# A selective-scan stage whose loop runs over batches instead of over batch and scan order

## What is computed

```python
x_dbl = einsum('bkdl,kcd->bkcl', xs, x_proj_w)         # -> dts (6), Bs (16), Cs (16)
delta = softplus(einsum('bkrl,kdr->bkdl', dts, dt_projs_w) + dt_projs_b)
A = -exp(A_logs)                                       # (K, 192, 16)
h = exp(delta * A) * h + (delta * u) * B               # 4096 steps, state 192 x 16
y = einsum('bkdn,bkn->bkd', h, C) + D * u
```

## Time and profile before

| | us |
|---|---|
| median of 3 runs (lowest, highest) | 13187.52 (13180.49, 13191.48) |
| the profiled execution's own time | 13188.5 |
| its span, first to last instruction | 13186.6 |
| scan stage, first to last recurrence | about 925 to 11000 |

### The profile page before, as it was taken

How to read it: one execution, slowest core, us unless ns; L and a number is a source line. 1 busy time by engine, 2 the same in 40 slices (tenths; PEclk the granted TensorE clock), 3 DMA queues, 4 the chain that set the end, 5 groups by cost and what they waited for, 6 DMA issues and landing times. The chain is left out here.

```text
span 13186.6 us, 117417 instructions
## 1 busy us (share of the span) xinstructions
PE 8944.7 (68%) x25624; PEld 2522.6 (19%) x25624; DVE 11097.4 (84%) x7002; ACT 7096.2 (54%) x9476; POOL 9937.2 (75%) x4196
## 2 busy tenths in 40 slices
PE   7866666666666666666666666666666664777777
PEld 2211111111111111111111111111111111222222
DVE  7769999999999999999999999999999995333333
ACT  6755555555555555555555555555555552444444
POOL 0029999999999999999999999999999994211220
PEclk9977777777777777777777777777777776888888
DMA  4567777777777777777777777777777784323230
GB/s 140 166 184 172 175 176 179 175 173 173 177 177 177 175 172 178 177 176 176 172 171 176 175 177 177 172 176 177 177 177 173 175 180 105 78 61 83 65 81 24
DMA packets 581902, 2060.69 MB, mean 156 GB/s; under 512 B 82662, under 2 KB 87654, under 8 KB 566886
## 3 DMA queue, kind: packets, MB, share of 16 engines
q1 hardware_dynamic: 581478, 2057.01, 68.1%
HBM read 1599.54 MB, written 457.18 MB: 156 GB/s over the span
## 5 line engine op out<-in xcount | busy, mean ns | idle before, releaser
L819 POOL TENSOR_TENSOR dBu<-rep,BC 128x1024 f32<-128x1024 f32 x3072 | 7152.8, 2354 | 963.0 <-DMA rep<-dd_dram 922.2
L615 PE MATMUL py<-hC,fold 128*32 128x512 f32 x12288 | 2958.3, 861 | 2587.5 <-POOL hC L826 2443.7
L664 ACT ACTIVATE pd<-rep,a_now 128x1024 f32<-128x1024 f32 x3072 | 3420.9, 1114 | 1326.4 <-DVE hC L787 1002.3
L779 DVE TENSOR_TENSOR_SCAN pd<-pd,carry,dBu 128x1024 f32<-128x1024 f32 x1536 | 3595.5, 2341 | 0.0
L826 POOL TENSOR_TENSOR hC<-h,BC 128x1024 f32<-128x1024 f32 x1024 | 2400.5, 2344 | 531.9 <-DVE h L779 484.7
L787 DVE TENSOR_TENSOR hC<-pd,BC 128x1024 f32<-128x1024 f32 x2048 | 2507.5, 1224 | 169.6 <-DVE pd L779 29.2
L779 DVE TENSOR_TENSOR_SCAN h<-pd,carry,dBu 128x1024 f32<-128x1024 f32 x768 | 1797.9, 2341 | 0.0
L676 ACT ACTIVATE carry<-pd 128x1 f32<-128x1 f32 x1536 | 262.0, 171 | 2630.2 <-DVE hC L787 2582.3
L615 PEld LDWEIGHTS py<-hC,fold 128*32 128x32 f32 x12288 | 516.8, 138 | 4803.9 <-POOL hC L826 3205.8
L779 DVE TENSOR_TENSOR_SCAN pd<-pd,dBu 128x1024 f32<-128x1024 f32 x512 | 1168.0, 2281 | 43.4 <-issue 28.3
L1385 POOL TENSOR_TENSOR p_yn<-p_yn,p_z 96x1024 f32<-96x1024 f32 x64 | 149.8, 2345 | 1192.3 <-DMA p_z<-zs_dram 774.8
(11 more groups left out here) (147 smaller groups left out, 9216.5 us busy)
## 6 DMA issues: line engine op xcount, KB each, us to landing
rep<-dd_dram SPq DMA_DIRECT2D x1024, 768.0 KB, 12.7
BC<-bc_dram SPq DMA_DIRECT2D x2048, 256.0 KB, 9.1
u_dram<-p_u SPq DMA_DIRECT2D x64, 1536.0 KB, 16.7
u<-u_dram SPq DMA_DIRECT2D x128, 768.0 KB, 5.4
dd_dram<-LG SPq DMA_DIRECT2D x256, 384.0 KB, 4.5
dd_dram<-RL SPq DMA_DIRECT2D x256, 384.0 KB, 3.0
y_dram<-y SPq DMA_DIRECT2D x256, 384.0 KB, 10.9
p_y<-y_dram SPq DMA_DIRECT2D x64, 1536.0 KB, 13.9
```

The lines of the kernel that those rows point to most:

```text
L615: last = mm(py[32 * g:32 * g + 32, t2(t)], fold[:, :], hC[:, j % 2 * 3 + g, t2(t)], start=(j % 4 == 0), stop=(j % 4 == 3), skip_group_chec ...
L664: go(pd[:, i % 2, :], rep[:, half, 0, g, :], ACT.Exp, scale=a_now[:, i:i + 1]).then_inc(S.exped, 1)
L779: v.tensor_tensor_scan(dst, pd[:, i % 2, :], dBu[:, i % 4, :], carry[:, i:i + 1] if c else 0.0, ALU.mult, ALU.add).then_inc(S.scanned, 1)
L819: nc.gpsimd.tensor_tensor(dBu[:, i % 4, :], rep[:, half, 1, g, :], BC[:, s, 0, r, :], ALU.mult).then_inc(S.dbu, 1)
```

## The change

The loop now runs over 7 batches. Its body has the four orders and so 16 chunks written out; the last batch, with its 4 orders, stands behind the loop. The bodies get the order's number `k` as a plain number, and `pick_a` uses it for the column of `a_neg`, whose address is then fixed and not computed from the loop's register. One `sem_inc` that stood between a wait and the copy in `pick_a` goes away. Of the 31 passages between orders, 6 are now jumps, 24 lie inside the written-out code and one leads out of the loop.

```diff
         def chunk_loop(eng, body):
 
-            with eng.Fori(0, BK - 1) as bk:
+            with eng.Fori(0, B - 1) as b:
+                for k in range(K):
+                    for c in range(NC):
+                        body(b * K + k, k, c, NC)
+            for k in range(K):
                 for c in range(NC):
-                    body(bk, c, NC)
-            for c in range(NC):
-                body(BK - 1, c, NC - 1 - c)
+                    body(BK - K + k, k, c, NC if k < K - 1 else NC - 1 - c)
...
-            def pick_a(bk):
+            def pick_a(bk, k):
                 act.wait_ge(S.exped, done(bk * NC * NS))
-                act.sem_inc(S.passed, 1)
-                go(a_now[:, :], a_neg[:, bk % K, :], ACT.Identity).then_inc(S.a_picked, 1)
+                go(a_now[:, :], a_neg[:, k, :], ACT.Identity).then_inc(S.a_picked, 1)
                 act.wait_ge(S.a_picked, done(bk + 1))
...
-            pick_a(0)
+            pick_a(0, 0)
...
-                            pick_a(bk + 1)
+                            pick_a(bk + 1, (k + 1) % K)
```

More of the change, by code:

```diff
@@ L533, in _, with body @@
             store_prep(0, 1)
-            def body(bk, c, left):
+            def body(bk, k, c, left):
                 n, s = bk * NC + c, c % 2
```

## The result

The changed kernel takes 13069.01 us (median of 4 runs, 13060.03 to 13072.89) against 13189.5 us (13180.49 to 13203.46) for the kernel before (also of four runs, the three given above among them): a ratio of 0.9907, with a 95% interval of 0.989 to 0.9924. That is 120 us less; 115 were forecast, and the forecast time of 13073 us is 4 us off. The profiled execution took 13060.03 us.

What follows compares the result with a forecast made beforehand. The prediction took DVE to bound the scan stage, losing 7.01 us at each passage between orders. Passages (105.0 us) plus constants (9.7) gave 114.7 us off, so 13073 us, 0.87% less, range 13030 to 13125.

Steps and rivals of the forecast that it cites:

- The jump's price, 3.65 us: Passage between orders: DVE loses 7.84 us with a jump, 4.19 on the way out of the loop, so 3.65 per jump.
- What stays at a straight passage, 2.7 us: Passages without a jump: DVE's remaining wait for PE, taken as 2.7 us at 25 passages, bounds 0.99 and 4.19.
- The middle kind: Passages where PE's clock level changes while it makes x_dbl: 6.33 us lost at a jump, 2.68 expected without one.
- The old price at the jumps that stay, 7.01 us: The 6 remaining jumps: each still costs DVE the earlier mean of 7.01 us, together 42.1 us.
- Sum of the passages: DVE's waits over all 31 passages between orders: 214.6 us before, 109.6 after, a gain of 105.0 us.
- Constants, 9.7 us: Chunks behind the loop, 16 in place of 4: 12 save 0.81 us each without semaphore values computed from the loop's register.
- The fixed address, 0: ACT's `pick_a`: one register instruction of 0.10 us less per order, at most 3.1 us if all exposed, taken as 0.
- The longer body, 0: Instruction loading for the longer loop body: straight code is loaded ahead in time, so it costs nothing.
- The time of the joints is not the jump's: Rival: ACT's idle pieces come from the order's start and stay in straight code; about 13178 us; 3 in 100.
- The register arithmetic grows: Rival: DVE's idle pieces double in 112 loop chunks, 91 us; the gain shrinks to 24, time 13165; 4 in 100.
- Loading stalls in straight code: Rival: instruction loads exposed on DVE or ACT, 2.3 us each; one per chunk gives about 13367 us; 4 in 100.

Runs made afterwards that it cites:

- two_orders: Kernel before with a loop body of two orders (8 chunks), the last two orders behind the loop, 14 jumps back: 13119.22 us, ratio 0.994.
- the shifts: Kernel before with 6 or 64 semaphore increments without effect in ACT's stream ahead of the loop: 13154.49 us (ratio 0.9964) and 13143.7 us (0.9955).
- unrolled: Changed kernel with no loop in the scan stage, 32 orders written out, all semaphore values constant: 12979.79 us, ratio to the kernel before 0.9845.
- constants_only: Kernel before, its one-order loop run over 28 orders with the last four behind it, 27 jumps: 13175.95 us, ratio 0.9984.
- address_only: Kernel before, one-order loop kept, with fixed column 0 of A in `pick_a` for all orders: 13190.96 us, ratio 0.9995.
- copy_later_one_order: Kernel before with first order ahead of the loop, `copy_y` and SP's store moved to the next chunk's tile 2 at every passage: 13016.54 us, ratio 0.9869.
- before_reduce_first: Kernel before with PE's last reduction ahead of `make_x_dbl` in each order's last chunk, 30 jumps kept: 13113.46 us, ratio 0.9935.

## Why the prediction was right, and how far

- *The jump's price, 3.65 us, read from the one passage that was none.* Right in kind, and 0.2 us low: the 6 jumps in the changed kernel cost DVE some 6.4 us each (1.48 + 4.87 in the timeline) and straight passages in the loop with the same x_dbl 2.47, so a jump is worth 3.9 us. The passage that I took for a straight one ran into the code with constants and so carried a little of their effect (next point). `two_orders` confirms that the number of jumps sets the time, and the shifts and the packets that it is a wait for instructions.
- *What stays at a straight passage, 2.7 us.* The middle kind measured 2.47 in the loop and 2.68 on the way out and behind it, where a small idle piece of DVE ahead of its first product goes (0.25 us), so that it reaches its third scan sooner and waits longer. The other kinds came unevenly: none of the passages had the quick x_dbl, and three had the one at the lower clock (3.9 to 4.2 us). The 25 passages sum to 67.2 us against 67.5 forecast, but that this is so close is luck: those three made up for a middle kind that I had 0.2 us too high. `unrolled` had eight such passages of 31, and 3.1 us on average.
- *The old price at the jumps that stay, 7.01 us.* Too high by 0.6, and this is most of the 4 us by which the passages gave more than forecast. The 7.01 were a mean over jumps of several kinds: of the 30 before, 14 cost 6.33 us, eight with an x_dbl of 6.6 to 7.0 us 7.9, six with a long piece 8.2, and two with a quick x_dbl 4.6. All six jumps of the changed kernel were of the first kind. The long pieces were there in kernels with the one-order loop (5.2 us in `constants_only`), not at the 14 jumps of `two_orders` (2.7 at most). They go with an instruction packet that comes over a microsecond late; what delays it is open.
- *Sum of the passages.* A gain of 105.0 us was forecast, and 214.6 - 105.4 = 109.2 measured.
- *Constants, 9.7 us.* Right: 76.58 against 77.39 us a chunk, twelve chunks. 109.2 + 9.7 = 118.9 of the stage's 120.6. That the time of the runs came within 4 us of the forecast is in part luck too, since what follows the stage alone varies by 20 us.
- *The fixed address, 0.* Right (`address_only`).
- *The longer body, 0.* Right for DVE's time. It did cost: POOL now idles up to 0.8 us on "issue" at each of the six jumps, and q8's packets went from 25 to 187. Behind the branch back, POOL (287 instructions a body before) and SP (320) went on after 0.20 to 0.27 us; with bodies of 1142 and 1275 they took 2.55 to 2.82 and 3.21 to 3.26 us, while ACT with its 505 had taken over 2.3 already. None of it shows in DVE's waits. PE's wait right behind the jump was 8.59 us against 8.55, so a load of its own, if it had one, lay under it.
- *The rivals.* "The time of the joints is not the jump's" is refuted by `two_orders` and the shifts, "The register arithmetic grows" by the chunk's 77.39 us, "Loading stalls in straight code" by the changed kernel itself and by `unrolled`, where not one wait of DVE inside an order is left.

What the prediction left out is that the price was avoidable in other ways. It said that `copy_y` ahead of the exponential is the rest of a passage's price; it is the reason for all of it but the late first scan (`copy_later_one_order`: 38.2 us left of 210.4). And in `before_reduce_first` I expected an earlier `copy_y` to hide the pieces without working out when the reduction can start.

## What to carry to other kernels

A loop's jump can cost an engine a wait for instructions: here ACT idled 1.6 us with nothing to wait for, or 3.9 by where the body stands in its stream, while POOL and SP with bodies of 287 and 320 instructions went on after 0.2 to 0.3 us. It shows in the time only where that engine reaches the jump last. So look first at what stands just ahead of the jump on the late engine: moving that wait (13017 us with 29 jumps) did more than a body four times as long (13069 us with 6). Price a joint from the one time that the loop is left, kind by kind and not by the mean, and expect a freed piece to come back in part when what is next late, here x_dbl, changes its own duration.

## What was not expected of the hardware

- Six semaphore increments ahead of a loop made the kernel 45 us faster, by removing a piece of 2.3 us, and at some jumps up to 5.4, at each of 30 jumps.
- Where its semaphore values are register sums, VectorE loses 0.81 us in a chunk of 77, although its instructions are long. Over the 112 chunks that `unrolled` takes out of the loop that is 91 us, three quarters of what the loop over batches won. The cause is read from the code and from where the time goes.
- The same 8 matrix products took 3.60, 5.29 and 6.82 us at three passages, at a granted clock of 1.00 (the 2.4 GHz level), with a change of level inside, and at 0.52, nearly all at the 1.2 GHz level (the earlier trace rows for the ends).
